# SiLU of x and SiLU of the gate rows in two ACT blocks, each with table loads of its own, in a software-pipelined selective-scan and expert-mixing kernel

## What is computed

```python
# first block: a selective scan
h = norm(x) @ w_in
xs, res = split(h)                      # 512 channels each
res = silu(res)                         # the gate rows
xs  = silu(causal_depthwise_conv(xs))   # 4 taps
delta, B, C = split(xs @ w_xproj)       # 16 + 16 + 16
delta = softplus(delta @ w_dt + b_dt)
# h[t] = exp(delta*A) * h[t-1] + (delta*xs)*B, for 16 states n, along the tokens
y = sum_n h_n * C_n
x = x + layernorm(x_in + ((y + xs*D) * res) @ w_out)
# second block: eight experts, two branches
# router: gelu, softmax; experts: (x V) * cumsum(x W), gated, times U
x = x + layernorm(experts(x))
```

## Time and profile before

| | us |
|---|---|
| median of 3 runs | 2413.68 (2412.34 to 2414.4) |
| profiled execution | 2413.96 |
| its span, first to last instruction | 2412.2 |
| busy in the span: PE | 2143.7 |
| DVE | 2147.9 |
| ACT | 1839.0 |
| POOL | 1898.4 |
| table loads, 65 of 1.283 us each | 83.4 |

### The profile page before, as it was taken

How to read it: one execution, slowest core, us unless ns; L and a number is a source line. 1 busy time by engine, 2 the same in 40 slices (tenths; PEclk the granted TensorE clock), 3 DMA queues, 4 the chain that set the end, 5 groups by cost and what they waited for, 6 DMA issues and landing times.

```text
span 2412.2 us, 35956 instructions
## 1 busy us (share of the span) xinstructions
PE 2143.7 (89%) x9268; PEld 1300.3 (54%) x9268; DVE 2147.9 (89%) x2775; ACT 1839.0 (76%) x3893; POOL 1898.4 (79%) x1369
## 2 busy tenths in 40 slices
PE   5687899999998989899998999999898999998888
PEld 2455455564655556465655646565564656555454
DVE  2889999998999999999999989999999999999920
ACT  6675787869698787968778696978879797875644
POOL 1679797988889798888979888897988889796520
PEclk8796899898999989999999989999899999989899
DMA  6111101111111011111102011110211110011000
GB/s 135 36 45 39 45 32 32 58 31 54 37 57 33 27 61 30 54 36 58 33 27 62 30 52 37 58 36 23 64 32 54 36 58 31 26 51 35 27 9 9
DMA packets 83401, 101.70 MB, mean 42 GB/s; under 512 B 23480, under 2 KB 49872, under 8 KB 83168
## 3 DMA queue, kind: packets, MB, share of 16 engines
q1 hardware_dynamic: 83168, 99.06, 13.7%
HBM read 90.13 MB, written 8.91 MB: 41 GB/s over the span
## 4 chain that ended last, share of the span: by engine, by line
DVE 34%; issue 26%; PE 15%; ACT 13%; POOL 9%; DVEq 1%; ACTq 0%; POOLq 0%
DVE h L1425 15%; DVE yT L1441 11%; PE bank L827 7%; POOL bx L792 4%; PE stateT L1007 4%; ACT decay L1277 2%; DVE xs L1336 2%; PE bank L986 1%; DVE yT L1438 1%; POOL dx L718 1%; POOL delta L712 1%; ACT scratch L1207 1%; ACT res L1141 1%; ACT prodT L1064 1%; ACT o_rows L1045 1%
## 5 line engine op out<-in xcount | busy, mean ns | idle before, releaser
L792 POOL TENSOR_TENSOR bx<-dx,B_rows 128x1024 f32<-128x1024 f32 x512 | 1204.6, 2363 | 286.9 <-DVE h L1425 252.4
L1425 DVE TENSOR_TENSOR_SCAN h<-decay,bx 128x512 f32<-128x512 f32 x1024 | 1236.8, 1208 | 64.7 <-ACT decay L1277 51.9
L1277 ACT ACTIVATE decay<-delta,decay_rate 128x512 f32<-128x512 f32 x1024 | 702.4, 691 | 351.0 <-DVE h L1425 343.0
L1007 PE MATMUL stateT<-ident,h 128*128 128x128 f32 x4096 | 646.9, 291 | 176.2 <-DVE h L1425 119.3
L1007 PEld LDWEIGHTS stateT<-ident,h 128*128 128x128 f32 x4096 | 492.6, 148 | 523.4 <-issue 306.8
L1441 DVE SCALAR_TENSOR_TENSOR yT<-stateT,C_tok,yT 128x512 f32<-128x512 f32 x960 | 694.7, 724 | 47.7 <-PE stateT L1007 47.5
L827 PE MATMUL bank<-hT,w_in_sb 128*128 128x512 f32 x512 | 246.5, 611 | 23.5 <-DVE xs L1336 9.9
L827 PE MATMUL bank<-q_to_expert,xnT 128*128 128x512 f32 x512 | 261.5, 638 | 0.1
L827 PE MATMUL bank<-k_to_expert,cumT 128*128 128x512 f32 x512 | 258.4, 630 | 0.0
L986 PE MATMUL bank<-expert_to_out,prodT 128*128 128x256 f32 x1024 | 244.5, 382 | 6.4 <-issue 6.4
L1241 ACT ACTIVATE cum_sb<-bank,gate 128x64 f32<-128x64 f32 x1024 | 221.8, 326 | 22.9 <-PE bank L827 20.2
(11 more groups left out here) (164 smaller groups left out, 2584.8 us busy)
## 6 DMA issues: line engine op xcount, KB each, us to landing
B_rows<-B_scratch SPq DMA_DIRECT2D x256, 256.0 KB, 3.2
x_front<-in_L_attn_x SPq DMA_DIRECT2D x16, 512.0 KB, 5.3
x_back<-in_L_attn_x SPq DMA_DIRECT2D x16, 512.0 KB, 3.5
out<-x_back SPq DMA_DIRECT2D x16, 512.0 KB, 5.8
w_in_sb<-in_L_attn_w_in SPq DMA_DIRECT2D x1, 1024.0 KB, 5.9
cum_sb<-in_L_ffn_V_fwd SPq DMA_DIRECT2D x2, 256.0 KB
prod<-in_L_ffn_W_inv_exp SPq DMA_DIRECT2D x2, 256.0 KB
xnT<-in_L_ffn_W_fwd SPq DMA_DIRECT2D x2, 256.0 KB
```

The costliest lines, as they stand in the source:

```text
L792: pool.tensor_tensor(bx[use % BX_RING][:, :, :], dx[q.parity][:, 2 * half:2 * half + 2, :], row, ALU.mult).then_inc(s_bx.step(f"{n},{half} ...
L1007: last = pe.transpose(stateT[j % 2][:, c * P:(c + 1) * P], h[n % 2][:, c, j * P:(j + 1) * P], ident[:, :])
L1277: act.activation(decay[c % 2][:, :], delta[q.parity][:, c, :], ACT.Exp, scale=decay_rate[:, c, n:n + 1]).then_inc(s_exp.step(f"{n},{c}"), 1)
L1425: dve.tensor_tensor_scan(h[n % 2][:, c, :], decay[c % 2][:, :], bx[(2 * n + c // 2) % BX_RING][:, c % 2, :], 0.0, ALU.mult, ALU.add).then_ ...
```

## The change

The task `F.silu` becomes two. `F.silux` keeps the wait for the convolution and the SiLU of `xs`, at beat 66 of ACT instead of 67, and loads the exp set right behind it. `F.silur` does SiLU of `res` at beat 120, with both table loads of its own. Stage F of a sequence thus has four table loads on ACT where it had two, and a period six where it had four. For the first sequence `silur` runs on its own behind all the `F.ln` tasks and ahead of the first `decay`. All beats were planned anew; most moved by one to four, some by more (`F.dt` of channel tile 3 on ACT from 108 to 115, `L.pr` of rows 0 on DVE from 99 to 108, `B.lb` from 88 to 84, the loading of the next x from 89 to 98 on SP).

```diff
 TIMETABLE = {
...
-    ("F", "silu", "act"): (67,),
+    ("F", "silux", "act"): (66,),
+    ("F", "silur", "act"): (120,),
...
-    ("F", "dt", "act"): (86, 90, 104, 108),
+    ("F", "dt", "act"): (86, 92, 104, 115),
...
-            def silu_task(b, k, use):
+            def silux_task(b, k, use):
                 if b.is_first:
-                    act.wait_ge(f_act.sem, f_act.done(b, "res3"))
-                    act.activation(res[b.parity][:, :, :], res[b.parity][:, :, :], ACT.Silu).then_inc(first_silu, 1)
                     act.preload_act_table_set(EXP_SET)
                     act.wait_ge(f_pe.sem, f_pe.done(b, "proj"))
-                    act.wait_ge(first_silu, 2)
+                    act.wait_ge(first_silu, 1)
                     act.sem_inc(f_act.step("silux"), 1)
-                    act.sem_inc(f_act.step("silur"), 1)
                     return
                 act.wait_ge(f_dve.sem, f_dve.done(b, "cvC2"))
                 act.wait_ge(f_pool.sem, f_pool.done(b, "cv33"))
                 act.sem_inc(passed["act"], 1)
                 act.preload_act_table_set("silu_and_others")
                 act.activation(xs[b.parity][:, :, :], xs[b.parity][:, :, :], ACT.Silu).then_inc(f_act.step("silux"), 1)
+                act.preload_act_table_set(EXP_SET)
+
+            def silur_task(b, k, use):
                 act.wait_ge(f_act.sem, f_act.done(b, "res3"))
+                act.sem_inc(passed["act"], 1)
+                act.preload_act_table_set("silu_and_others")
                 act.activation(res[b.parity][:, :, :], res[b.parity][:, :, :], ACT.Silu).then_inc(f_act.step("silur"), 1)
                 act.preload_act_table_set(EXP_SET)
```

More of the change, by code:

```diff
@@ L129 @@
-    ("B", "u", "dve"): (264, 264, 269, 271),
-    ("B", "o", "pool"): (273, 275, 276, 279),
-    ("B", "wo", "pe"): (279, 281, 284, 288),
-    ("B", "r", "dve"): (285, 289, 290, 291),
+    ("F", "cvC", "dve"): (36, None, 39, None),
+    ("F", "tap", "act"): (None, 37, None, 43),
+    ("F", "cv", "pool"): (None, 39, None, 63),
+    ("F", "res", "pe"): (38, 43, 44, 54),
+    ("F", "res", "act"): (44, 45, 49, 61),
+    ("F", "silux", "act"): (66,),
+    ("F", "silur", "act"): (120,),
+    ("F", "proj", "pe"): (76,),
@@ new lines @@
+    ("F", "proj", "act"): (82,),
+    ("F", "B", "sp"): (80,),
+    ("F", "Ct", "pe"): (119,),
+    ("F", "Ct", "act"): (120,),
+    ("F", "dt", "pe"): (82, 87, 93, 107),
+    ("F", "dt", "act"): (86, 92, 104, 115),
+    ("F", "ex", "act"): (89, 95, 106, 116),
+    ("F", "ln", "act"): (91, 96, 111, 118),
+    ("F", "w", "pool"): (96, 105, 120, 121),
+    ("F", "w2", "pool"): (101, 111, 123, 126),
+    ("F", "d1", "pool"): (104, 118, 126, 128),
+    ("F", "row", "sp"): (108, 119, 130),
+    ("B", "y", "pe"): (264, 265, 266, 266),
@@ L140 @@
-    ("B", "rb1", "pool"): (319,),
+    ("B", "st1", "dve"): (308,),
+    ("B", "ag1", "dve"): (309,),
+    ("B", "rb1", "pool"): (318,),
     ("B", "xn", "act"): (314,),
-    ("B", "xnT", "pe"): (315, 316),
-    ("B", "xnT", "act"): (319, 320),
-    ("B", "cum", "dve"): (323, 323),
-    ("B", "rt", "pe"): (324, 325, 327, 329),
-    ("B", "rt", "act"): (327, 329, 332, 333),
+    ("B", "xnT", "pe"): (316, 318),
+    ("B", "xnT", "act"): (319, 321),
+    ("B", "cum", "dve"): (321, 322),
+    ("B", "rt", "pe"): (320, 325, 326, 328),
@@ L149 @@
     ("B", "logit", "act"): (340,),
[L150 to L153 removed]
+    ("B", "logit_rows", "pe"): (339,),
+    ("B", "lb", "dve"): (340,),
+    ("B", "mx", "dve"): (341,),
+    ("B", "sub", "pool"): (348,),
     ("B", "ex", "act"): (347,),
[L155 to L157 removed]
+    ("B", "sm", "dve"): (348,),
+    ("B", "sn", "pool"): (356,),
+    ("B", "rc", "dve"): (348,),
     ("B", "wa", "pool"): (358,),
[L159 to L163 removed]
[4 rows of a table removed]
[L168 to L170 removed]
+    ("B", "gT", "pe"): (356,),
+    ("B", "gT", "act"): (358,),
+    ("L", "cum", "pe"): (344, 346, 358, 375, 382, 390, 403, 434),
+    ("L", "xv", "pe"): (355, 366, 368, 376, 397, 422, 431, 435),
+    ("L", "cum", "act"): (354, 356, 368, 378, 388, 392, 409, 436),
[4 rows of a table added]
+    ("L", "out", "act"): (388, 403, 446, 452),
+    ("L", "sq", "act"): (455,),
+    ("L", "rs", "pool"): (460,),
     ("L", "t", "act"): (466,),
[L172 removed]
+    ("F", "dx", "pool"): (116, 120, 128, 130),
     ("L", "x", "pool"): (472, 472),
[L174 removed]
+    ("L", "store", "sp"): (479,),
 }
@@ L319, in program @@
                                                        "Ct": ["Ct"], "dt": ["dt{}"]}))
-        f_act = Steps(sem("f_act"), steps_of("act", "F", {"sum": numbered("sm"), "sq": numbered("sq"), "h": numbered("h"), "hT": ["hT{}"], "xs": ["cv{}"], "tap": ["tp{}1", "tp{}2", "tp{}3"], "res": ["res{}"], "silu": ["silux", "silur"],
+        f_act = Steps(sem("f_act"), steps_of("act", "F", {"sum": numbered("sm"), "sq": numbered("sq"), "h": numbered("h"), "hT": ["hT{}"], "xs": ["cv{}"], "tap": ["tp{}1", "tp{}2", "tp{}3"], "res": ["res{}"], "silux": ["silux"], "silur": ["silur"],
                                                           "proj": ["proj"], "Ct": ["Ct"], "dt": ["ab{}", "rl{}"], "ex": ["ex{}", "v{}"], "ln": ["ln{}", "u{}"]}))
```

64 lines of the change are left out of this document (16 added, 48 removed), and 8 rows, old and new, of the table TIMETABLE.

## The result

| us | before | after |
|---|---|---|
| median of 6 runs each | 2413.01 (2411.8 to 2414.66) | 2421.94 (2419.99 to 2423.6) |
| profiled execution, its span | 2413.96, 2412.2 | 2419.99, 2418.2 |
| one period, from a scan in the loop to the same scan eleven periods later | 139.9 | 140.6 |
| mean granted clock of TensorE over the span | 0.941 | 0.942 |

The ratio is 1.0036, with a 95% interval of 1.0023 to 1.0049: the changed kernel is 8.9 us slower. DVE's work did not change (2147.9 and 2149.3 us), so the difference lies in its waits. These are the same ten periods as in the earlier trace rows, in the trace of after; the columns are total us, times, longest.

The account below looks back on a forecast made before the run. DVE bounds the kernel: 133.1 us of work and 6.8 of waits in a 139.9 us period. Terms -1.45 + 1.4 + 0 - 0.1 + 0.15 + 0 = 0.0 a period, with the start +1 us: 2415, range 2392 to 2438.

Parts of the forecast that it names:

- First block, -1.45 a period: SiLU block near beat 66: shortened from 6.32 to 4.52 us, DVE's wait of 1.45 us for decay behind it goes.
- Second block, +1.4: New SiLU block of res at beat 120: DVE waits 1.4 us at beat 122's scan, between 0 and 3.2.
- the second block is hidden, 2394: Rival at beat 120: ACT's 4.4 us idle hold the block, DVE waits 0; 2394 us, chance 0.09.
- GELU, 0: GELU block: DVE's waits of 0.47 and 1.66 us stay, as its neighbours on ACT are the same; 0.
- Beats, -0.1: Beats 84 to 90: accumulation may wait 0.25 us, a wait of 0.35 may go; -0.1, between -0.35 and +0.6.
- POOL, +0.15 at the edge: Period's edge, beat 4: later softplus input adds 0.3 us to the bx wait in every second period, +0.15.
- TensorE's clock, 0 between -1.8 and +1.2: DVE's waits for stateT behind low-clock stretches of PE: no net change a period, between -1.8 and +1.2 us.
- Start, +1 once: First sequence: silur ahead of the first decay delays the first scans; +1 us once, between 0 and +2.5.
- The rival of the clock staying up, 2396: Near beat 105: PE's shorter gaps keep the clock up, the 1.26 us wait goes each period; 2396 us, chance 0.19.
- ACT without a lead, 2442: Rival at beat 122's scan: ACT has no lead at the second block, wait 3.2 instead of 1.4; 2442 us, chance 0.22.
- The table loads: Added ACT loads cost 1.28 us each; the skill's 2.66 us a switch would give 2456 us, chance 0.01.

Follow-up runs that it names:

- its filling alone: Changed kernel with the matmuls of dt0 and dt3 run twice and stateT's transposes twice at beats 106, 108, 110: 2399.50 us, ratio 0.9947.
- the filled kernel before: Kernel before with a full 128x128 by 128x512 matmul ahead of dt0 and dt1, dt3 twice, stateT's transposes twice at beats 98 to 106: 2398.60 us.
- the fills: Changed kernel with added TensorE work: a full matmul ahead of dt0 and dt1, dt3 twice, stateT's transposes twice at beats 106, 108, 110: 2378.39 us.

## Why the prediction was right, point by point

The forecast was 2415 with a range of 2392 to 2438; the time is 2421.94, a change of 8.9 us where 1 was forecast, inside the forecast's own 2405 to 2425. It lies outside the 2408.9 to 2418.5 that I called no change, and of the directions slower had 0.37 and faster 0.38. That the time stayed so near the forecast is in part luck: the clock's term, taken as 0, came to 10.3 us in ten periods, and 2.4 us at the GELU block and 2.7 us ahead of the first scan, neither of which I had, took a part of it back. The range of 46 us is wide against a change of 9.

- *First block, -1.45 a period*: right, to the hundredth, and for the reason given: DVE's prefix sums end last.
- *Second block, +1.4*: measured 1.32. Adding up ACT's and DVE's work gave the size, and it also gave 3.5 for the split at the old beats (3.43 measured). The sum began at the wrong scan, though: I said ACT would be busy without a break for 13 us, and it stood idle for 0.77 us ahead of the decay at 1162.79, 8.4 us before the scan. Counted from there (the scan of beat 114), the same terms give 9.5 us for ACT and 8.3 for DVE, again 1.2. And the run with the block left out shows that it was wrong to read this wait as a price: in ten periods 6.0 of 13.2 us go when it goes, and 9.5 us of the time. The rival "the second block is hidden, 2394" could not have paid what I wrote.
- *GELU, 0*: 2.13 went to 1.90, -2.4 us in ten periods that I did not have; no run shows what took it away.
- *Beats, -0.1*: the accumulation at beat 85 waits 0.31 (0.25 expected), the decay near beat 90 no longer does (-0.35): both right, and with one period of 0.61 at beat 85 they come to 0 for the -0.1.
- *POOL, +0.15 at the edge*: `bx` waits as before, 0.36. What I left out of my list of waits is that in every other second period DVE waits 1.0 to 1.5 us at the edge in before; that wait, 6.2 us in ten periods, is 7.5 after, and so the edge grew by 0.12 a period all the same.
- *TensorE's clock, 0 between -1.8 and +1.2*: this is the term that was mis-sized. It is +1.0 a period, 10.3 us in ten, nearly at the upper bound. The clock was low for as long as before (108 windows of 1 us for 105); what I had not priced is which wait stands behind each stretch. I looked at the stretch at beats 102 to 110 alone, which the earlier trace rows show, and said of beats 86 to 95 only that a wait there would make me wrong. In before the clock fell there in six of ten periods. The changed order makes it nine of ten, and puts `L.cum0` and its `stateT` behind the fall, so that the wait is up to 2.0 and not 1.2. The new gap ahead of the logits was named in the prediction, but its filling alone left the clock falling there in all ten periods; what TensorE computed there did change it. At the stretch of beats 102 to 110 I took the wait of 1.26 for the price of the clock; the filled kernel before shows a wait of 0.77 for `decay` behind it.
- *Start, +1 once*: I had the first scan at 65.6 for 65.02. It came at 63.44, since DVE was done with the step sizes earlier, but the scans behind it waited for `decay`. The first SiLU in the loop started at 132.16 before and 132.06 after, so about 0.
- *The rival of the clock staying up, 2396*, did not happen by itself. Made to happen by the fills, it gave 2378, 43.5 us and so more than the 18.9 I had put on it, since both stretches carry waits.
- *ACT without a lead, 2442*: did not happen, as the idle 0.77 us of ACT show. The 3.43 at the old beats looks like it, but ACT had its lead there too (idle for 0.88 us ahead of the block); it was `L.cum3` behind the block that made the wait.
- *The table loads*: each took 1.28 us and the next instruction started 0.01 us behind it, also with three in a row, and a pair more cost the scan 2.57 at the block. The Trainium skill, "ScalarE: Activation LUTs", section "What ACT_TABLE_LOAD costs", counts about 2.66 us for a switch with its drain; the traces here show no drain beside the loads, so the 2456 that I had put beside this figure did not come.

The sum of the terms as measured, -14.5 + 13.2 - 2.4 + 0 + 10.3 + 1.2 in ten periods, is +7.8, against 8.9 by the medians and 6.0 by the two profiled executions. To multiply by 1.5 for fifteen sequences, as I did in the forecast, would give 11.7 and does not hold: from 70 to 400 us and from 1796 us on DVE's waits are the same in both traces (128.0 and 128.2 us), and before 70 us they are 2.7 less after.

## What to carry to other kernels

When the order of work moves on several engines, look at every stretch in which TensorE's granted clock falls, also those that fall only in some periods, and ask which waiting engine stands behind it; here that term was larger than the net of all others, though the clock was low for no longer. A wait that is seen at one engine says what its removal may give, not what it gives: ask which engine is late next, and test it by leaving the work out. In the changed kernel the waits for `stateT` gave all that they showed (28.6 of 29.1 us), the wait at the second block under half (6.0 of 13.2), and in the kernel before a low clock stretch about 0.4 of 1.2, with a wait for ACT right behind it. And where a block on one engine is moved, count the lead it can use up from the last release, not the idle time of the window around it.
